# Expert tiles as loops on the engines, and a first feed-forward stage with its tokens in one part

## The reference

```python
# layer 0: shared experts for every token, two routed experts out of eight
h_sh = gelu(einsum('bsd,nfd->bsnf', x, Wfc_sh)); shared_out = einsum('bsnf,ndf->bsd', h_sh, Wproj_sh)
expert_out = gelu(x @ Wfc_r[e].T) @ Wproj_r[e].T        # for each of the two chosen e
return x + shared_out + sum(weight[e] * expert_out[e])  # weights: softmax of two sigmoids
# layer 1: two routed experts out of eight, with biases
h = gelu(x @ W1[e] + b1[e]); y = h @ W2[e] + b2[e]; output = output + y * combine_w[e]
```

## Time and profile before

| what | us |
|---|---|
| median of three runs | 1457.05 (1453.18 to 1457.63) |
| the profiled execution, its own time | 1444.6 |
| its span, from the first to the last instruction | 1442.8 |
| TensorE busy | 1175.6 |
| VectorE, ScalarE, GpSimd busy | 829.6, 649.3, 600.1 |

### The profile page before, as it was taken

How to read it: one execution, slowest core, us unless ns; L and a number is a source line. 1 busy time by engine, 2 the same in 40 slices (tenths; PEclk the granted TensorE clock), 3 DMA queues, 4 the chain that set the end, 5 groups by cost and what they waited for, 6 DMA issues and landing times. The chain is left out here.

```text
span 1442.8 us, 31655 instructions
## 1 busy us (share of the span) xinstructions
PE 1175.6 (81%) x11702; PEld 988.7 (69%) x11702; DVE 829.6 (57%) x1805; ACT 649.3 (45%) x1171; POOL 600.1 (42%) x622
## 2 busy tenths in 40 slices
PE   6979989919996889689999999968997718886840
PEld 4766666819996867468888888856767718885840
DVE  6859978403221324358888888847986615553541
ACT  5327754304453424155666656536772103452410
POOL 4742323264444235544343433333342463444255
PEclk9999998959997999899999999999997959997975
DMA  6002215012221121100000000001105011221122
GB/s 171 9 2 66 51 24 202 14 46 49 57 65 47 46 85 32 44 6 1 0 0 0 0 0 0 1 6 19 21 9 196 25 45 43 60 58 46 42 79 69
DMA packets 61906, 62.62 MB, mean 43 GB/s; under 512 B 12592, under 2 KB 50864, under 8 KB 61296
## 3 DMA queue, kind: packets, MB, share of 16 engines
q1 hardware_dynamic: 51824, 42.52, 9.9%
q0 software_dynamic: 9088, 18.63, 5.2%
q10 hardware_dynamic: 896, 0.17, 0.1%
HBM read 42.67 MB, written 16.52 MB: 41 GB/s over the span
## 5 line engine op out<-in xcount | busy, mean ns | idle before, releaser
L1963 PE MATMUL f_bank<-f_xT,f_w_tile 128*128 128x128 f32 x1248 | 184.5, 295 | 82.7 <-issue 48.1
L1963 PEld LDWEIGHTS f_bank<-f_xT,f_w_tile 128*128 128x128 f32 x1248 | 167.7, 208 | 88.9 <-issue 50.8
L1975 PE MATMUL f_bank<-f_w_down,f_hidden 128*128 x1248 | 179.2, 290 | 50.8 <-ACT f_hidden L1880 30.0
L1975 PEld LDWEIGHTS f_bank<-f_w_down,f_hidden 128*128 128x128 f32 x1248 | 162.6, 203 | 56.4 <-issue 56.2
L1616 POOL DMA_INDIRECT f_xn<-f_xn_rows,f_source x156 | 148.6, 952 | 47.4 <-issue 47.4
L1424 POOL TENSOR_TENSOR f_turn_cell<-ident 128x1 f32<-128x1 f32 x60 | 12.8, 213 | 319.5 <-issue 107.1
L1627 POOL DMA_INDIRECT f_hot_row<-f_slots_y,f_slots x128 | 122.6, 958 | 39.9 <-issue 39.9
L1050 POOL TENSOR_TENSOR ret_rstd<-ret_var,ret_minus_half 128x8 f32<-128x8 f32 x32 | 52.7, 1647 | 173.5 <-DVE ret_var L1089 173.5
L1880 ACT ACTIVATE f_hidden<-f_before_gelu 128x512 f32<-128x512 f32 x78 | 49.0, 629 | 162.0 <-DVE f_before_gelu L1802 146.4
L1880 ACT ACTIVATE f_hidden<-f_bank 128x512 f32<-128x512 f32 x78 | 46.5, 596 | 149.5 <-remote 83.9
L1868 ACT ACTIVATE f_w_tile<-f_w_up 128x512 f32 x156 | 96.2, 619 | 29.0 <-DVE f_owner L1768 28.2
(11 more groups left out here) (283 smaller groups left out, 2827.8 us busy)
## 6 DMA issues: line engine op xcount, KB each, us to landing
f_slots_y<-f_y_out SPq DMA_DIRECT2D x76, 128.0 KB
a_v_rows<-in_ctx SPq DMA_DIRECT2D x16, 256.0 KB, 4.0
f_xn_rows<-f_xn SPq DMA_DIRECT2D x16, 256.0 KB
f_w_up<-in_f_up SPq DMA_DIRECT2D x1, 2560.0 KB, 10.1
f_w_down<-in_f_down SPq DMA_DIRECT2D x1, 2560.0 KB, 17.1
f_xn<-f_xn_rows,f_source POOLq DMA_INDIRECT x156
X<-in_x SPq DMA_DIRECT2D x4, 512.0 KB, 5.3
kv_ctxT<-in_ctxT SPq DMA_DIRECT2D x8, 256.0 KB, 5.7
```

What stands on the lines that cost most here:

```text
L1963: last = pe.matmul(bank_h[m % 2][:, j * P:(j + 1) * P], w_tile[m % W_RING][:, j * P:(j + 1) * P], xT[m % 2][:], start=True, stop=True)
L1975: last = pe.matmul(bank_y[m % 2][:, 0:D].unsqueeze(1), hidden[m % 2][:, j, :], w_down[:, bass.ds(expert + E0, 1), j, :], start=(j == 0), s ...
```

## The change

The diff, cut to its core. The tile steps of all three engines become a head, a loop over bodies of eight tiles, and a tail. ScalarE copies the gathered tile to one of four staging buffers, and SyncE waits for the gathers and counts them. `y_out` becomes one buffer of eight tiles, the weights have two buffers instead of three. `ffn0` has one part (71 slot tiles), four units in front and twelve behind. In `ffn1` GpSimd does one of the two operations on `hot_tile` for the groups ahead of the tiles, the steps for the later groups are 4, 8, 12, and four groups are added between the tiles, from steps 58, 63, 68 and 73.

```diff
-W_RING = 3
-FIRST_UNITS = 6
+BODY = STORED * Y_RING
+W_RING, X_RING = 2, 4
+FIRST_UNITS = 4
...
+    BY_POOL, ADDED_AT = range(first_group[1]) if spec["last"] else (), spec["added_at"]
+    HOT_LATER, SOURCES_AT = ((4, 8, 12), 15) if parts > 1 else ((), None)
+    dve_loop, act_loop, pe_loop = spec["loops"]
...
-        def owner_of(kind, tile):
+        def owners(kind, tile, count=1):
...
+        def over_tiles(eng, step, begin, end):
+            for s in range(begin):
+                step(s, s % BODY, s)
+            with eng.Fori(begin // BODY, end // BODY) as i:
+                for k in range(BODY):
+                    step(BODY * i + k, k, None, i)
+            for s in range(end, M + 2):
+                step(s, s % BODY, s)
...
+                for q in range(-(-M // STORED)):
+                    while ahead < len(lots) and lots[ahead][0] <= STORED * q + BODY:
+                        sp.wait_ge(landed[ahead], landed_base[ahead] + 16 * lots[ahead][1])
+                        sp.sem_inc(S["rows_landed"], lots[ahead][1])
+                        ahead += 1
...
+                for q in BY_POOL:
+                    pool.wait_ge(S["hot_tile_set"], q + 1)
...
+                    pool.tensor_tensor(out, out, token_rows[:, at].unsqueeze(1).unsqueeze(3).to_broadcast(shape),
+                                       ALU.mult).then_inc(S["hot_tile_ready"], 1)
...
-                    waits = [(S["source_ready"], part_of[begin] + 1), (S["xT_in_psum"], begin + size - RING)]
+                    waits = [(S["source_ready"], part_of[begin] + 1), (S["x_staged"], begin + size - RING)]
...
+                    if biased and tile is None:
+                        if k == 0:
+                            held.update(zip(range(-4, 0), owners(mybir.EngineType.DVE, s - 4, 4)))
+                        if k == 1:
+                            held.update(zip(range(BODY), owners(mybir.EngineType.DVE, s - 1, BODY)))
...
+                                if k == 0:
+                                    held.update(zip(range(BODY), owners(mybir.EngineType.Activation, s, BODY)))
+                                if k == BODY - 1:
+                                    held[BODY], = owners(mybir.EngineType.Activation, s + 1)
+                                expert = held[k + 1]
+                            copy_weights(s + t, (k + t) % W_RING, expert)
+                    for t in (0, 1, 2) if tile == 0 else (2,):
...
+                            act.wait_ge(S["rows_landed"], s + t + 1)
+                            need(act, S["xT_in_psum"], s + t - X_RING + 1)
+                            nc.scalar.activation(x_stage[(k + t) % X_RING][:].unsqueeze(1), x_in[:, bass.ds(slot, 1), :],
+                                                 ACT.Copy).then_inc(S["x_staged"], 1)
...
-                    COLLECT = {(3, "up"): (0,), (3, "down"): (1,), (4, "up"): (2, 3), (4, "down"): (4, 5),
-                               (5, "up"): (6,), (5, "down"): (7,)}
+                    COLLECT = {(3, "up"): (0,), (3, "down"): (1, 2), (4, "up"): (3,), (4, "down"): (4, 5, 6, 7)}
...
+                            if j == 1 and tile is None and k == 0:
+                                held.update({(back, "loop"): value for back, value in
+                                             zip(range(-4, 0), owners(mybir.EngineType.PE, s - 4, 4))})
+                            if j == 1 and tile is None and k == 1:
+                                held.update({(back, "loop"): value for back, value in
+                                             zip(range(BODY), owners(mybir.EngineType.PE, s - 1, BODY))})
...
-HOT_LATER = (4, 10, 16)
-ADDED_AT = (63, 69, 75)
...
-    ffn_phase(g, "f0", dict(kind="sigmoid", plus_xn=True, part_tiles=(20, 12), last=False, shared=2, following=weights, gelu=ACT.Gelu, gate_w="f0_gate_w",
+    ffn_phase(g, "f0", dict(kind="sigmoid", plus_xn=True, part_tiles=(TILES,), last=False, shared=2, following=weights, added_at=(),
+                            loops=((8, 64), (8, 64), (8, 64)), gelu=ACT.Gelu, gate_w="f0_gate_w",
...
-    ffn_phase(g, "f1", dict(kind="softmax", plus_xn=False, part_tiles=(20, 12), last=True, shared=0, following=None, gelu=ACT.Gelu_apprx_tanh,
+    ffn_phase(g, "f1", dict(kind="softmax", plus_xn=False, part_tiles=(20, 12), last=True, shared=0, following=None, added_at=(58, 63, 68, 73),
+                            loops=((16, 56), (8, 72), (16, 72)), gelu=ACT.Gelu_apprx_tanh,
```

More of the change, by code:

```diff
@@ L1818, in _ @@
                         ins.then_inc(S["y_ready"], 1)
-                    if parts > 1 and s in HOT_LATER:
-                        hot(first_group[1] + HOT_LATER.index(s))
-                        if s == HOT_LATER[-1]:
-                            sources(1)
-                    if parts > 1:
-                        for m, begin in enumerate(ADDED_AT):
-                            if s in range(begin, begin + 4):
-                                add_rows(dve, m, s - begin)
+                    if tile in HOT_LATER:
+                        hot(first_group[1] + HOT_LATER.index(tile))
+                    if tile is not None and tile == SOURCES_AT:
+                        sources(1)
+                    for m, begin in enumerate(ADDED_AT):
+                        if tile is not None and tile in range(begin, begin + 4):
+                            add_rows(dve, m, tile - begin)
+                over_tiles(dve, step, *dve_loop)
                 for m in range(GROUPS):
@@ L1869, in copy_weights, with step @@
                         .then_inc(S["w_ready"], 1)
[L1871 to L1877 removed]
+                def step(s, k, tile, i=None):
+                    m, b = s - 1, (k - 1) % 2
+                    if live(m, M):
                         act.wait_ge(S["biased"] if biased else S["up_done"], m + 1)
@@ L1883, in _ @@
+                over_tiles(act, step, *act_loop)
                 if shared:
```

167 lines of the change are left out of this document (94 added, 73 removed).

## The result

The changed kernel takes 1474.25 us (median of four runs, 1471.51 to 1477.08) against 1455.74 for the kernel before in the same comparison (1453.18 to 1457.63): a ratio of 1.0128, 95% interval 1.0101 to 1.0156. It is **slower by 1.3%**, 18.5 us, where 1451 and a small gain were forecast. The time lies inside the range of 1426 to 1476 and close to the 1476 of rival C, but not for C's reason, as the first rows and the run `e1_unrolled` show; that closeness is chance.

What follows compares the result with a forecast made beforehand. The bound was taken to be TensorE's hand-off while GpSimd's gathers run back to back. First stage -8.9 and second +3.1 gave -5.8 us, 1438.8 for the profiled execution, scaled to 1451; range 1426 to 1476.

Steps and rivals of the forecast that it cites:

- rival C: Both stages' loop bodies: twelve TensorE register loads of 0.30 us open gaps, +19 us in all, 1476; chance 0.25.
- Rival A: Both feed-forward stages: the change works as summed, 1451 us, own range 1442 to 1460; chance 0.40.
- B: First-stage tail: shared experts' matmuls are not blocked by 32 gathers; +16 us in place of +39, 1428; chance 0.20.
- D: First-stage tail: units 4 and 5 slip through, giving a run of 40 gathers; +8 us, 1459; chance 0.11.
- E: Blocked stretches in both stages are instruction loading, which loops remove; -66 us in all, 1391; chance 0.04.
- Items 1, 3, 4, 5: First-stage tiles, us: fewer tiles -13.3, later groups and lots -8.8, no result gathers between tiles -31.3, loops +1.5.
- Item 2: In front of the first-stage tiles: all eight one-hot groups, costed as VectorE operations, +4 us (0 to +9).
- Item 6: Behind first-stage tiles: two more units +14 us, TensorE blocked beside 32 back-to-back gathers +25 (0 to 33); +39.
- The signs named: First-stage tail: some 25 us idle TensorE, ScalarE marked "remote", ended 2 to 5 us after the 32nd gather.
- The adding of a fourth group: Second stage: a third run of eight gathers falls among the tiles, +2.1 us.
- the x stage: Tile steps: the staging copy and SyncE's waits stand several tiles ahead of their users, so they cost nothing.

Runs made afterwards that it cites:

- e1_unrolled: Changed kernel with every tile step of both stages unrolled; ratio 1.0120 to the kernel before.
- e11: e8 with two more shared-expert units between the collecting matmuls and the tiles, ten left behind; ratio 1.0024 to the kernel before.
- e9: Kernel before with four groups added between the second stage's tiles, from steps 58, 63, 68 and 73, instead of three; ratio 0.9999.
- e7: First stage of the kernel before, second stage of the changed kernel; ratio 1.0065 to the kernel before.
- e10: e7 with the second stage unrolled and without the staging copy, SyncE's counting and their waits; ratio 1.0002 to the kernel before.
- e18: Kernel before with two tiny GpSimd operations behind gathers of rows and of results, adding moved to steps 68, 72, 76; 1320.9 us, ratio 0.9143.
- e4: Changed kernel with first-stage gathers of groups 2 to 7 waiting for shared units, so no run exceeds 16; ratio 1.0133 to the kernel before.
- e6: Changed kernel, unchanged, traced again on the same chip as e5; span 1458.7 us.
- e8: First stage of the changed kernel, second stage of the kernel before; ratio 1.0065 to the kernel before.
- e12: e11 with gathers of groups 2, 4 and 6 waiting for 2, 5 and 8 units of the tail; ratio 1.0045 to the kernel before.
- e16: Kernel before with three tiny GpSimd operations behind each gather of rows for the tiles, both stages; 1388.3 us, ratio 0.9505.
- e15: e8 with three tiny GpSimd operations behind each gather of groups 0 to 3 in the first stage; ratio 1.0080 to the kernel before.
- before: Kernel before, unchanged, in the profiled execution the prediction was made from; 1444.6 us.
- e5: Kernel before, unchanged, traced again on the same chip as e6; span 1442.8 us.
- e3: Changed kernel with the first stage back to two parts and six units in front, loops and staging kept; ratio 1.0119 to the kernel before.
- e13: e8 with the first stage's tile steps unrolled and without the staging copy; ratio 1.0077 to the kernel before.

## Why the prediction was wrong

- **Sign.** The forecast -5.8 us for the profiled execution was +15.9 on one chip. Rival A's mechanism is right in its main parts; three of its terms were too small. The part of rival C's forecast that came true is the number only: e1 and the 24 tiles in 45.5 us show no cost of loads or branches. B fell (units were not at 7.00 throughout), and D as well (in one part with four units, group 4 started after a gap; with six, in e11, 40 gathers did run back to back). E fell: the hold-ups stay with loops, and no instructions were being loaded in the longest.
- **Items 1, 3, 4, 5**, -51.9: measured -51.0, with errors of -2.5 and +3.5 in it that cancel.
- **Item 2, the step that failed first.** "A group grows from about 2.2 us to 2.7. Three more are 8.1": the groups were costed on VectorE. But TensorE was without a gap in that part. There the three groups cost 5.5 us, the wider operands 0.6 and two waits for VectorE 2.0, less 3.5 for the up projection that is gone: some +4.6, near the +4 by another path, which is luck. What made +11.0 of it is a term that the sum does not have at all, the fall of TensorE's granted clock among the collecting matmuls, some 6.3. The prediction has no row of TensorE's busy time or clock in front of the source.
- **Item 6, mis-sized.** +39 was 14 + 25; measured 51.1, of which 14 for two units and 37.2 for hold-ups, above the upper bound of 33. It did work on for 16.6 us behind the last copy, as said, but "with a hand-off slipping through now and then I take 25" failed: its own matmuls stand as well, and the first run cost 30.4, above the 29 given as the most. The prediction also left out that groups 6 and 7 make a second run of 16, 6.8 us. The signs named were otherwise seen: "remote" on ScalarE and the release 5 us after the end of the 32nd gather.
- **Second stage.** The adding of a fourth group was costed at +2.1; e9 gives -0.1, with 2.5 us either way, which does not refute it. That the x stage costs "nothing" was the error: it is the whole 9.4 us by time (e7 against e10), and by rows at least 5. It was costed by its cover (ScalarE has time) and not by the hand-off it adds to the ring.
- **The hold-up taken as given.** Item 2 ("the tiles wait for the gathers anyway, and are blocked by them until they end") and the whole tail took it so. Spacing the gathers, with the adding moved later, is worth some 120 us of the kernel before (e18), and was the thing to change.

## What to carry to other kernels

Where a feed of small indirect DMAs from GpSimd goes back to back and TensorE's timeline beside it shows single matmuls with "issue", or other engines show "remote", try a break between them: less than one microsecond each, with the adding moved later, was worth 8.6% here. The break makes GpSimd late, so what waits for its gathers has to move as well. Cost a moved group on every engine that touches it, the one without idle time first. And a copy that only decouples two engines is not free where its hand-off stands in the loop that feeds the gathers.

## What the runs showed of the hardware

- Indirect DMAs of 128 rows issued 1.25 us apart hold TensorE up from 13 to 14 us after the first one on (e4, e6, e8, e11; 18 in the last run of e6). Its instructions then start 0.7 to 2.8 us apart, even those that wait for nothing, and its granted clock falls (0.61 from 493.7 to 530 in e6). It is not the volume: the DMA queues moved 43 GB/s in that stretch, and up to 364 from 480 to 489, when TensorE was not held up. For the shared units, runs of eight did no harm (e4), runs of 16 cost 7 to 11 us (e4, e6, e8, e12), runs of 32 about 30 (e6, e8). The tile steps are more sensitive: in e16 TensorE stands 4.0, 1.5 and 3.4 us with "issue" beside runs of eight.
- With 0.6 to 1.0 us between them instead of 0.30, TensorE is busy 32.0 of 34.2 us in e15 and 55.0 of 57.4 in e18. What the shared resource is, no run here shows.
- TensorE's granted clock falls among the collecting matmuls: 0.64 from 267.0 to 275.4 in e6, 0.80 in `before`, e7 and e9, 1.00 in e5 and e10. `before` and e5 are the same kernel, so it is not fixed by the program.
- One load instruction on TensorE's sequencer brings eight values to registers in 0.59 to 0.88 us, four in 0.33 to 0.35, one in 0.30.
- Between executions of the same kernel e1, e3, e7 and e13 scatter over 13 to 15 us, the kernel before over 11, e18 over 4. The reason is open.
